# The last layer norm moved into the expert tiles of a decoder layer

## The reference

```python
gate = softmax(xf @ gate_w + gate_b)              # 8 experts
topv, topi = top_k(gate, 2)                       # two experts per token, weights normalised to 1
combine = (one_hot(topi, 8) * topv[..., None]).sum(1)
def body(acc, p):
    h = relu(xf @ w1e + b1e)                      # 256 -> 1024
    y = h @ w2e + b2e                             # 1024 -> 256
    return acc + y * ce[:, None]
out = scan(body, 0, experts)                      # sum over the experts
x = layernorm(x + out)                            # (x - mean) / sqrt(var + eps), row by row
```

## Time and profile before

| | before |
|---|---|
| median of 3 runs | 1484.65 us (1484.28 to 1486.24) |
| time of the profiled execution | 1487.28 us |
| span of its instructions | 1485.5 us |
| busy in the span: PE, DVE, ACT, POOL | 95%, 65%, 58%, 26% |
| DMA, mean over the span | 89 GB/s |

### The profile page before, as it was taken

How to read it: one execution, slowest core, us unless ns; L and a number is a source line. 1 busy time by engine, 2 the same in 40 slices (tenths; PEclk the granted TensorE clock), 3 DMA queues, 4 the chain that set the end, 5 groups by cost and what they waited for, 6 DMA issues and landing times.

```text
span 1485.5 us, 47820 instructions
## 1 busy us (share of the span) xinstructions
PE 1407.7 (95%) x18566; PEld 929.3 (63%) x18566; DVE 967.9 (65%) x1679; ACT 860.7 (58%) x1966; POOL 388.2 (26%) x677
## 2 busy tenths in 40 slices
PE   7999999999999999999999988999999999999990
PEld 3344444544445445444444448889999999999980
DVE  6777888888888898888999944555333333333326
ACT  3477788887877777778778772333333333333320
POOL 1211121212222225321234112454522222222223
PEclk9799999999999999999999999999999999999995
DMA  5324232434344324322523243224322222222216
GB/s 160 93 69 140 72 91 88 126 110 128 115 122 144 88 68 130 110 63 69 160 88 110 59 151 77 58 73 104 76 47 39 37 37 37 37 37 40 39 21 230
DMA packets 112254, 131.55 MB, mean 89 GB/s; under 512 B 26048, under 2 KB 89808, under 8 KB 111904
## 3 DMA queue, kind: packets, MB, share of 16 engines
q1 hardware_dynamic: 93760, 101.68, 23.1%
q0 software_dynamic: 14000, 19.48, 7.4%
q10 hardware_dynamic: 4272, 7.34, 1.4%
HBM read 76.51 MB, written 51.94 MB: 86 GB/s over the span
## 4 chain that ended last, share of the span: by engine, by line
PE 82%; DVE 8%; issue 3%; DMA 3%; ACT 2%; SPq 1%; DVEq 0%; POOL 0%; POOLq 0%; ACTq 0%
PE pa L1071 16%; PE pb L1082 16%; PE pa L853 13%; PE pb L853 12%; PE po L1020 12%; PE px L853 6%; DVE neg L1343 4%; PE px L846 2%; ACT w_sb L1155 1%; PE po L949 1%; PE px L924 1%; PE pb L846 1%; SPq L607 1%; PE px L899 1%; DVE w_sb L1784 1%
## 5 line engine op out<-in xcount | busy, mean ns | idle before, releaser
L1155 ACT ACTIVATE w_sb<-pb 128x512 f32<-128x512 f32 x996 | 590.0, 599 | 135.2 <-PE pb L853 99.2
L1343 DVE TENSOR_REDUCE neg<-pa 128x1 f32<-128x1024 f32 x512 | 612.4, 1214 | 85.0 <-PE pa L853 77.8
L853 PE MATMUL pb<-w_sb 99*32 99x512 bf16 x3984 | 393.1, 381 | 3.9 <-ACT w_sb L1155 1.5
L1268 ACT ACTIVATE space<-pa,b1T_sb 128x128 f32<-128x128 f32 x568 | 154.8, 383 | 329.8 <-PE pa L1071 329.8
L853 PE MATMUL pa<-w_sb 96*32 96x512 bf16 (+1 forms) x4208 | 328.1, 385 | 11.1 <-DVE neg L1343 10.5
L1020 PE MATMUL po<-w_sb,space 128*32 128x256 f32 x4096 | 311.9, 379 | 0.1
L1071 PE MATMUL pa<-xgT,attn_t 128*128 128x128 f32 x2272 | 270.3, 276 | 9.7 <-DVE attn_t L1687 9.7
L1071 PEld LDWEIGHTS pa<-xgT,attn_t 128*128 128x128 f32 x2272 | 267.8, 193 | 13.8 <-issue 10.3
L1082 PE MATMUL pb<-w_sb,space 128*128 x1136 | 261.3, 381 | 0.0
L1082 PEld LDWEIGHTS pb<-w_sb,space 128*128 128x128 f32 x1136 | 209.8, 191 | 25.1
L802 POOL DMA_INDIRECT x<-space,y_tag x71 | 110.7, 1559 | 364.7 <-DVE space L1704 297.3
(11 more groups left out here) (209 smaller groups left out, 961.6 us busy)
## 6 DMA issues: line engine op xcount, KB each, us to landing
xg<-x_by_expert SPq DMA_DIRECT2D x71, 130.0 KB, 2.4
attention_out<-space SPq DMA_DIRECT2D x64, 128.0 KB, 2.0
w_sb<-w SPq DMA_DIRECT2D x16, 512.0 KB, 5.1
q_parts<-w_sb SPq DMA_DIRECT2D x48, 128.0 KB
w_sb<-q_parts SPq DMA_DIRECT2D x64, 96.0 KB, 2.6
w_sb<-k_parts SPq DMA_DIRECT2D x64, 96.0 KB, 2.8
k_parts<-w_sb SPq DMA_DIRECT2D x45, 128.0 KB
w_sb<-w SPq DMA_DIRECT2D x5, 1024.0 KB, 8.4
```

The lines of the kernel that those rows point to most:

```text
L853: mm = pe.matmul(out[at:end], lhsT[:, at:end], rhs, start=start, stop=stop, tile_position=(0, at))
L1155: act.activation(ex[:, n % 4, half * HALF:(half + 1) * HALF], score_bank(n, half), ACT.Exp, scale=SCALE).then_inc(e_done, 1)
L1268: ins = act.activation(hT[tile % 2][:, f, :], pH[tile % 2][:, f, :], ACT.Relu, bias=g.b1_sb[:, bass.ds(e * FT + f, 1)])
L1343: dve.tensor_reduce(neg[i % 2][:, t:t + 1], pa[n % 2][:, :], AX.X, ALU.max, negate=True).then_inc(max_done, 1)
```

## The change

The separate tail goes. Each expert tile now norms its own rows. For tile `t` POOL first gathers the tile's tokens' sums so far from `x2` into the on-chip buffer `x3` (`gather`); then it scatters the tile's results into `x2` with the add, as before (`scatter`). DVE adds the result to the gathered sums and takes the statistics (`measure_3`), POOL computes one over the standard deviation (`spread_3`), DVE norms (`norm_3`), and POOL scatters the normed rows to `out` (`scatter_out`, a plain indirect DMA). A token's rows are written to `out` twice, once by each of its two tiles, the second time with both results in the sum. `gather(t)` waits until `scatter(t - 1)` has landed; `scatter(t)` now also waits until `gather(t)` has landed, and `scatter_out(t)` until `scatter_out(t - 1)` has. `y_tag` gets 6 buffers and `out` gets the padding rows too, which the host cuts off. The 15 stores of zeros become 4 larger ones over 28 blocks of 128 rows.

```diff
-    TAGS = 4
-    GT = 4
-    NG = NT // GT
+    TAGS = 6
...
@@ SP
-                        for e in range(NE + SPARE):
-                            sp.dma_start(g.x2_dram[B * S + e * P:B * S + (e + 1) * P, :], spare_rows[:, 0, 0:D]
-                                         ).then_inc(dump_out, 16)
+                        for at in range(Y_ROWS - 4 * SPARE * P, Y_ROWS, SPARE * P):
+                            sp.dma_start(g.x2_dram[at:at + SPARE * P, :].rearrange("(k p) d -> p k d", p=P),
+                                         spare_rows[:, :, 0:D]).then_inc(dump_out, 16)
...
-                for i in range(TAGS):
-                    sp.wait_ge(y_out[i], 16 * len(range(i, FFN_TILES, TAGS)))
-                for n in range(NG):
-                    settle(sp, g.settled_dma)
-                    sp.dma_start(xr[:, n * GT:(n + 1) * GT, :], rows_of(g.x2_dram, n)).then_inc(sums_in[n], 16)
@@ POOL
-                def scatter(tile):
+                def gather(tile):
                     if tile == 0 or tile == EARLY:
                         for b in range(2) if tile == 0 else range(2, B):
                             pool.wait_ge(x2_out[b], 16 * TB)
-                    pool.wait_ge(result_done, tile + 1)
+                    pool.wait_ge(kept, tile + 1)
                     if tile:
                         pool.wait_ge(y_out[(tile - 1) % TAGS], 16 * ((tile - 1) // TAGS + 1))
+                    if tile >= 2:
+                        pool.wait_ge(out_rows, 16 * (tile - 1))
+                    settle(pool, settled_pool)
+                    pool.indirect_dma_start(x3[tile % 2], None, g.x2_dram,
+                                            bass.IndirectOffsetOnAxis(y_tag[tile % TAGS][:, 0:1], 0),
+                                            bounds_check=Y_ROWS - 1).then_inc(x3_in, 16)
+
+                def spread_3(tile):
+                    pool.wait_ge(c_aggr, tile + 1)
+                    pool.tensor_tensor(c_dev[:, :], c_mv[:, 1:2], eps[:, 0:1], ALU.add).then_inc(c_var, 1)
+                    pool.wait_ge(c_var, tile + 1)
+                    pool.tensor_tensor(c_rstd[:, :], c_dev[:, :], g.neg_half[:, 0:1], ALU.pow).then_inc(c_rstd_done, 1)
+
+                def scatter_out(tile):
+                    pool.wait_ge(c_normed, tile + 1)
+                    if tile:
+                        pool.wait_ge(out_rows, 16 * tile)
+                    settle(pool, settled_pool)
+                    pool.indirect_dma_start(g.out, bass.IndirectOffsetOnAxis(y_tag[tile % TAGS][:, 0:1], 0),
+                                            x3[tile % 2], None, bounds_check=Y_ROWS - 1).then_inc(out_rows, 16)
+
+                def scatter(tile):
+                    pool.wait_ge(result_done, tile + 1)
+                    pool.wait_ge(x3_in, 16 * (tile + 1))
                     settle(pool, settled_pool)
                     pool.indirect_dma_start(g.x2_dram, ..., y[tile % 2], None, compute_op=ALU.add).then_inc(y_out[tile % TAGS], 16)
...
                 for tile in range(FFN_TILES):
                     if tile == 1:
                         scale_heads(NH // PER - 1)
+                        pool.wait_ge(scaled, NH // PER)
+                        gather(0)
                     if tile:
                         scatter(tile - 1)
...
+                    if tile:
+                        spread_3(tile - 1)
+                        gather(tile)
+                        scatter_out(tile - 1)
-                scatter(FFN_TILES - 1)
-                ... (the tail's adds and powers, 8 groups)
+                spread_3(FFN_TILES - 1)
+                scatter_out(FFN_TILES - 1)
+                pool.wait_ge(out_rows, 16 * FFN_TILES)
@@ ACT: the eight stores to out and the wait for them go
@@ DVE
                 def keep(tile):
                     if tile >= TAGS:
                         dve.wait_ge(y_out[tile % TAGS], 16 * (tile // TAGS))
+                        dve.wait_ge(out_rows, 16 * (tile - TAGS + 1))
...
+                def measure_3(tile):
+                    z = x3[tile % 2]
+                    dve.wait_ge(result_done, tile + 1)
+                    dve.wait_ge(x3_in, 16 * (tile + 1))
+                    dve.tensor_tensor(z, z, y[tile % 2], ALU.add).then_inc(c_sum, 1)
+                    dve.wait_ge(c_sum, tile + 1)
+                    dve.bn_stats(c_stats[:, :], z).then_inc(c_stat, 1)
+                    dve.wait_ge(c_stat, tile + 1)
+                    settle(dve, g.settled)
+                    dve.bn_aggr(c_mv[:, :], c_stats[:, :]).then_inc(c_aggr, 1)
+
+                def norm_3(tile):
+                    z = x3[tile % 2]
+                    dve.wait_ge(c_rstd_done, tile + 1)
+                    dve.tensor_scalar(z, z, c_mv[:, 0:1], c_rstd[:, 0:1], ALU.subtract, ALU.mult).then_inc(c_normed, 1)
...
                     if tile + 2 < FFN_TILES:
                         e = number(dve, tile + 2, 1)
                         keep(tile + 2)
+                    if tile >= 2:
+                        measure_3(tile - 1)
                     ... (cross-attention's mix, then the two copies copy_w1(tile + 2, .))
                     if tile == 1:
                         result(0)
+                        measure_3(0)
+                    if tile:
+                        norm_3(tile - 1)
...
                 result(FFN_TILES - 1)
-                ... (the tail's statistics and norms, 8 groups)
+                measure_3(FFN_TILES - 1)
+                norm_3(FFN_TILES - 1)
```

More of the change, by code:

```diff
@@ L304, in stream @@
         xg = [sb(f"xg{i}", [P, PAYLOAD]) for i in range(XS)]
-        y_tag = [sb(f"y_tag{i}", [P, 2], I32) for i in range(TAGS)]
+        tags = sb("tags", [P, TAGS, 2], I32)
+        y_tag = [tags[:, i, :] for i in range(TAGS)]
         early_room, late_room = xg[2][:, :], x1[:, :, :].rearrange("p i d -> p (i d)")
@@ L310, in stream @@
         y = [spaces[2][:, i * D:(i + 1) * D] for i in range(2)]
[L311 to L314, removed]
+        x3 = [spaces[2][:, (2 + i) * D:(3 + i) * D] for i in range(2)]
+        c_all = sb("c_all", [P, 10])
+        c_stats, c_mv, c_dev, c_rstd = c_all[:, 0:6], c_all[:, 6:8], c_all[:, 8:9], c_all[:, 9:10]
         pa = [ps(f"pa{i}", [P, S]) for i in range(2)]
@@ L387, in stream @@
         settled_pool, settled_act = sem("settled_pool"), sem("settled_act")
-        sums_in = [sem(f"sums_in{n}") for n in range(NG)]
-        c_stat, c_aggr, c_var, c_rstd_done, c_normed, out_stored = (
-            sem(n) for n in ("c_stat", "c_aggr", "c_var", "c_rstd", "c_normed", "out_stored"))
+        x3_in, out_rows = sem("x3_in"), sem("out_rows")
+        c_sum, c_stat, c_aggr, c_var, c_rstd_done, c_normed = (
+            sem(n) for n in ("c_sum", "c_stat", "c_aggr", "c_var", "c_rstd_done", "c_normed"))
         def load_w2(eng, e):
@@ L605, in _ @@
                                      ).then_inc(spare_in, 16)
[L606 to L608 removed]
+                        for at in range(Y_ROWS - 4 * SPARE * P, Y_ROWS, SPARE * P):
+                            sp.dma_start(g.x2_dram[at:at + SPARE * P, :].rearrange("(k p) d -> p k d", p=P),
+                                         spare_rows[:, :, 0:D]).then_inc(dump_out, 16)
                     if i == 12:
[L610 removed]
+                        sp.wait_ge(dump_out, 16 * 4)
                     if H <= i < H + g.w1_loads:
@@ L1300, in _ @@
                         soft(j)
[L1301 to L1305, removed]
             @block.vector
@@ L1834 @@
              for n, v in arrays.items()}
-    out = nc.dram_tensor("out", (B * S, D), F32, kind="ExternalOutput").ap()
+    out = nc.dram_tensor("out", (Y_ROWS, D), F32, kind="ExternalOutput").ap()
     build_program(nc, **given, out=out)
     result = run_bass_kernel_spmd(nc, [arrays], core_ids=[0])
-    return result.results[0]["out"].reshape(B, S, D)
+    return result.results[0]["out"][0:B * S].reshape(B, S, D)
```

19 lines of the change are left out of this document (removed).

## The result

| | before | after |
|---|---|---|
| median of 4 runs, us | 1485.39 (1484.28 to 1486.24) | 1592.26 (1589.67 to 1594.5) |
| profiled execution, span, us | 1487.28, 1485.5 | 1592.95, 1590.8 |

The ratio is 1.0711, with a 95% interval of 1.0694 to 1.0728. The forecast was 1558 and its range 1516 to 1622: the sign and the range held, the centre was 34 us short.

A forecast was written before the change was run, and what follows sets the result against it. PE, always busy from 1090 to 1438 us, was taken as the bound, then an idle tail. Terms 65.8 + 24.6 + 12.3 + 1 − 30.4 = +73 us on 1484.65 gave 1558, range 1516 to 1622.

The forecast's parts named there:

- The ring: Every expert tile: gather and scatter wait for each other's landings, making a step 8.48 us instead of 7.24 after tile 19.
- the long stretch: Expert loop, steps 20 to 70, where PE was always busy: 51 steps, 432.5 us instead of 366.7, +65.8.
- The gather's landing: Each expert tile, gather's start to landing: 2.7 us, taken from the plain indirect scatter, bounds 2.4 and 3.9.
- Scatter to gather: Each expert tile, scatter's start to next gather's start: 4.68 us, plus 0.2 for DVE's copies (bounds 0 and 0.4).
- The second rival: Expert loop: DVE's copies stop descriptor making altogether, adding 1.3 to 1.55 us, step 9.7, 1620 us in all; chance 0.08.
- Steps 4 to 10: Expert loop: cross-attention's norms and two routed scatters precede the gather on POOL; 12.5 us a step, +12.3 in all.
- Steps 11 to 19: Expert loop: two scatters of routed rows precede the gather on POOL; 9.8 us a step, +24.6 in all.
- Steps 1 to 3: Start of the expert loop: steps already long, set by cross-attention's chain; +1 us.
- The end: After scatter 70 begins: a tail of 37.45 us goes, 7.1 us come in its place, a gain of 30.4.
- The slow gather: Expert loop: gather lands in 3.9 us or takes POOL 1.55; steps of 9.7, 1641 us in all; chance 0.15.
- the fast one: Expert loop: gather lands quickly, sum zero at 1.6 us; within PE's beat, full gain of 30 gives 1460; chance 0.06.
- The stopped descriptors: The second rival: DVE's copies stop POOL's descriptor making in the expert loop; step 9.7, 1620 us in all; chance 0.08.

The follow-up runs named there:

- the control: The changed kernel unaltered, measured again on the chip of the two versions with split copies: 1600.46 us, +115.2 us against the kernel before, ratio 1.0769.

## Why the prediction was right, and where it was short

**The ring.** Right, and shown by two runs: take it out, and the long stretch is back at 7.20; put in nothing else, and it is at 8.91. The cover of 1.8 us was gone as foretold, with PE standing still 1.35 us a step instead of 1.2.

**The gather's landing, the term that was mis-sized most.** From gather to next scatter 3.84 us instead of 2.7 + 0.9 = 3.6. I took the median of the plain scatter, 2.7, but that is this gather's shortest landing; its median is 2.9 and its longest 4.9, and a ring pays for each long one. The sum needs a mean, which is 2.97 in these 50 steps. 50 steps × 0.24 = 12 of the 15.8 us that were missing in the long stretch. The estimate by the Trainium skill's formula ("DMA: Bandwidth & Descriptors", section "Anatomy of one DMA — SWDGE (gpsimd) path"), 2.3 us, lies below the shortest that the trace shows.

**Scatter to gather.** 4.96 instead of 4.68 + 0.2: some 4 us in all. The scatter took 1.82 on POOL under DVE's copies, about what the one such row had said, and landed after 4.0 instead of 3.8. What the copies cost hangs on which begins first, which the prediction did not weigh. In after the scatter begins ahead of the copies and loses 0.2; with one copy behind it, it loses nothing (1.60). A plain scatter that begins under a copy loses 0.45 (1.44 with both copies on DVE, 1.45 with one), most of the 0.59 that is left of the copy which is running; a second copy behind that one adds nothing. The Trainium skill's rule on the shared port ("SBUF — State Buffer", section "SBUF: two separate sides") is that whichever of VectorE's two-port operation and GpSimd's starts first holds it for its whole instruction, and the other waits. The plain scatter agrees; the 0.2 of the adding one, which began first, this rule does not give. The second rival's step of 9.7 us, for which both copies would have to be added whole, is excluded by 8.80.

**Steps 4 to 10: right number, wrong reason.** 12.86 for 12.5. But cutting the ring left them at 13.1 and reordering POOL at 12.47. The step that failed: "DVE's own added work, five instructions, some 1.7 us a tile, has room". The room was there (DVE is busy 51 of the 90 us of these steps in after); the two waits were not weighed. That the number came out is luck. On DVE, the add waits for the gather ahead of the cross-attention's work, and `norm_3` waits for POOL's power ahead of the next result. The prediction had named only the copies as queued behind the add. The second of these waits is shown by a run, at 0.8 of the 2.35 us by which a step is longer with the ring cut; the first only by a chain, and its 3.0 us of waiting in seven steps leave most of the other 1.5 us a step open.

**Steps 11 to 19.** 10.09 for 9.8. With the ring cut they are at 9.3, with the power moved too at 9.1, and POOL is full: its own queue is 8.9 us long. The prediction said that POOL's queue counts here; it does, ahead of the landing and without it.

**Steps 1 to 3.** +4.0 for +1, 3 us short. They were given no working. They took 35.1 us with the gather alone, 36.0 with the ring cut and 33.1 with the power first as well, for 30.8 in before and 34.8 in after, so neither the ring nor the power alone is the cause; it stays open.

**The end.** 19.7 us from scatter 69 instead of 15.6, by two errors that partly cancel. I let scatter 70 be issued; the change drops it, since nobody reads its sums. And I let the span end with the last landing. This is the last issue on POOL, and what POOL does after it at the close of the block, a wait for the landing and a `DRAIN`:

```profile
1581.97 1.05 POOL L812 DMA_INDIRECT out<-space,tags  x1 [1.37 <-DVE space L1736]
...
L430 POOLq COMPARE_BRANCH  x1: 44/44/44, 1584.5 to 1584.5; - x1
...
L430 POOLq DRAIN  x1: 5950/5950/5950, 1584.7 to 1584.7; - x1
```

From the start of the last issue to the end of the span are 8.9 us: the landing has been waited for after 2.6, and the closing `DRAIN` takes 5.95 more. The tail of before also ended with such a `DRAIN` (1477.4 to 1485.2), which the prediction counted as going with the tail; in after it is there again.

**The rivals.** The slow gather (decides from 3.4 us on) and the fast one (from 1.6) are both excluded by a landing of 2.97 in the mean and 2.7 at the least; the gather took POOL 1.1 us, not 1.55. The stopped descriptors fell with the scatter's 1.82.

## What to carry to other kernels

Two dependent DMAs per iteration make a ring of two landings and two starts, here 8.8 us, and no engine's spare time shortens it; compare that ring with the loop's beat before anything else, and size it with mean landings. In the kernel without the waits (the ring cut) the same instructions and transfers took 7.2 us. For each wait that is added, list on both engines what stands behind it in order: here the add's wait for the gather held up the copies and, now and then, the cross-attention, and the norm's wait for POOL held up the next result. If a tail is to be shortened, first ask which engine sets its beat: moving one of its operations to an idle engine gave 5.7 us, and moving the whole tail into the loop lost 107.

## What was not expected of the hardware

- The end of a kernel after its last indirect DMA: 8.9 us to the span's end in after and in the control, 7.6 to 7.9 in the versions with a plain scatter. 5.95 of them, 4.7 to 5.0 in those versions, are POOL's closing `DRAIN`; in after no data move in it. What it waits for isn't in the trace.
- A plain indirect scatter that begins under a copy on DVE ends 0.86 us after that copy does, and takes 1.45 us on POOL instead of 0.99; one that adds and begins ahead of two copies takes 1.82 instead of 1.60.
- Moving both copies off DVE took 0.2 us off POOL's scatter (1.82 to 1.60), yet the gathers then took 3.31 us from start to use instead of 3.06, and the total stayed. Open.
- The same kernel before took 1511 us on two chips and 1485 on the others, with the difference ahead of the loop, and the same change cost 107 us in one comparison and 115 in another.
